# Unread TensorE products ahead of the waits in the last attention batch and ahead of the scan, with the last router logits moved

## What is computed

```python
x = x + mamba2(layernorm(x), ...)               # 64 heads of 64, state 128, convolution over 4 taps, gate, rmsnorm
x = x + cross_attention(layernorm(x), ctx, ...)  # 16 query heads of 128, 4 key heads, 64 context tokens per sequence
x = x + moe(layernorm(x), ...)                   # 8 experts, the best 2 of each token, plus 2 shared experts
```

## Time and profile before

| what | us |
| --- | --- |
| runs, median (lowest to highest, 3 runs) | 1702.9 (1699.85 to 1706.84) |
| the profiled execution, its own time | 1701.57 |
| its span, first to last instruction | 1699.8 |
| busy: TensorE products | 1608.0 |
| busy: VectorE | 1311.0 |
| busy: ScalarE | 1223.0 |
| busy: GpSimd | 601.8 |
| mean granted TensorE clock, share of full | 0.982 |

### The profile page before, as it was taken

One profiled execution on the slowest core, in us unless ns is written; L12 is line 12 of the kernel. 1 busy time (PEld: TensorE's weight loads), 2 busy tenths in 40 slices (PEclk: granted clock), 3 DMA queues, 4 the chain that ended last, 5 costly groups with the idle time before them and its releaser, 6 DMA issues. The chain is left out here.

```text
span 1699.8 us, 28898 instructions
## 1 busy us (share of the span) xinstructions
PE 1608.0 (95%) x9892; PEld 1286.0 (76%) x9892; DVE 1311.0 (77%) x2048; ACT 1223.0 (72%) x2531; POOL 601.8 (35%) x469
## 2 busy tenths in 40 slices
PE   5489999999999999999999999999968989999999
PEld 3367777777777777777777677877757889999888
DVE  7969999999999999999999865667657533333355
ACT  4679999999999999999999576566624324444331
POOL 1413343433434333333333411311121653334461
PEclk9679999999999999999999999999989999999999
DMA  8956444444444444444443100000104233223231
GB/s 321 393 226 246 171 150 173 150 153 170 151 172 149 154 169 151 166 156 155 169 152 147 56 1 1 2 1 2 47 29 146 90 131 116 90 92 112 81 94 56
DMA packets 74268, 220.30 MB, mean 130 GB/s; under 512 B 8848, under 2 KB 29584, under 8 KB 72464
## 3 DMA queue, kind: packets, MB, share of 16 engines
q1 hardware_dynamic: 68464, 192.38, 31.8%
q0 software_dynamic: 5664, 26.09, 4.4%
HBM read 184.62 MB, written 33.82 MB: 129 GB/s over the span
## 5 line engine op out<-in xcount | busy, mean ns | idle before, releaser
L624 POOL TENSOR_TENSOR m_gT<-m_gy,m_zs 128x512 f32<-128x512 f32 x128 | 166.5, 1301 | 534.4 <-DVE m_gy L794 534.4
L753 DVE SCALAR_TENSOR_TENSOR m_xc<-banks,k_cw,m_xc 128x510 f32<-128x510 f32 (+2 forms) x384 | 285.4, 743 | 15.0 <-ACT m_xc L665 5.9
L850 PE MATMUL banks<-pair_hi,m_wxz 128*128 128x512 f32 x680 | 243.5, 408 | 2.5 <-DMA m_wxz<-w_split 2.5
L893 PE MATMUL m_ps_out<-k_won,m_gT 128*128 128x256 f32 x1024 | 242.3, 379 | 3.6 <-POOL m_gT L624 2.0
L765 DVE TENSOR_TENSOR m_mat<-m_mat,k_cbm 128x768 f32<-128x768 f32 x256 | 232.5, 950 | 2.7 <-ACT m_mat L686 2.7
L893 PEld LDWEIGHTS m_ps_out<-k_won,m_gT 128*128 128x128 f32 x1024 | 193.7, 190 | 36.7 <-POOL m_gT L624 3.3
L881 PE MATMUL m_ps_y<-m_mat,m_xdt 128*64 128x256 f32 (+1 forms) x2048 | 194.7, 332 | 0.0
L686 ACT ACTIVATE m_mat<-m_mat 128x1536 f32<-128x1536 f32 x128 | 188.5, 1472 | 0.0
L881 PEld LDWEIGHTS m_ps_y<-m_mat,m_xdt 128*64 128x64 f32 x2048 | 126.8, 136 | 80.0 <-issue 42.3
L677 ACT ACTIVATE m_mat<-m_a_all,k_cum 128x256 f32<-128x256 f32 x340 | 170.5, 501 | 0.2 <-PE m_ps_y L881 0.2
L635 POOL TENSOR_TENSOR m_g_sum<-m_g_sum,m_g_sq 128x512 f32<-128x512 f32 x124 | 163.1, 1315 | 5.2 <-ACT m_g_sq L692 5.1
(11 more groups left out here) (307 smaller groups left out, 3691.5 us busy)
## 6 DMA issues: line engine op xcount, KB each, us to landing
m_wxz<-w_split SPq DMA_DIRECT2D x85, 512.0 KB, 3.4
m_a_all<-a_by_head SPq DMA_DIRECT2D x85, 512.0 KB, 4.3
k_w_first<-w_split SPq DMA_DIRECT2D x43, 512.0 KB, 3.4
k_a_first<-a_by_head SPq DMA_DIRECT2D x43, 512.0 KB, 4.3
w_split<-p_w_hl SPq DMA_DIRECT2D x15, 1024.0 KB, 8.7
raw<-in_w_gate_up POOLq DMA_DIRECT2D x9, 1280.0 KB, 6.4
raw<-in_w_xz SPq DMA_DIRECT2D x16, 512.0 KB, 7.2
raw<-in_w_down POOLq DMA_DIRECT2D x9, 640.0 KB, 7.7
```

The costliest lines, as they stand in the source:

```text
L624: pool.tensor_tensor(gT[:, n % 2, :], gy[:, n % 2, :], zs[:, n % 2, :], ALU.mult).then_inc(g_done, 1)
L753: dve.scalar_tensor_tensor(out=out[:, :, k:], in0=ps[:, :, 0:SEQ - k], scalar=cw[:, c, TAPS - 1 - k:TAPS - k], in1=out[:, :, k:], op0=ALU. ...
L850: last = pe.matmul(ps[:, :], w, a, start=m == 0, stop=m == len(terms) - 1)
L893: last = pe.matmul(ps_out[:, q * HID:(q + 1) * HID], gT[:, n % 2, q * P:(q + 1) * P], won[:, c, :], start=c == 0 and q % 2 == 0, stop=c == ...
```

## The change

TensorE's program alone is touched. In two stages it gets a helper `keep_warm(n)` that issues n products of tokens which lie in SBUF, into a PSUM tile that nobody reads again, without a semaphore. In `mamba_prepare` a product has 512 columns and goes into `ps_dt`; there are 12 of them before `c_times_b(2)`, 4 before `c_times_b(3)` and 5 after it, and ahead of the first stands a wait for both copies out of `ps_dt`. In `cross_attention_phase` a product has 256 columns and goes into `ps_q[0]`; in the last batch there are 18 before `scores(7, 1)`, 24 before `f_T(6)`, 14 before `probs_T(7, 0)` and 6 before `attend(7, 0)`. There `f_logits(6)` also moves from ahead of `probs_T(7, 1)` to behind it.

```diff
@@ mamba_prepare, tensor
+            def keep_warm(n):
+                for m in range(n):
+                    pe.matmul(ps_dt[:, 0:TG], xT_hi[:, 0, 0:P], xT_hi[:, 1, 0:TG], start=True, stop=True)
+
...
                 if m % CB == 1:
                     c_times_b(m // CB - 2)
+            pe.wait_ge(aT_done, 2)
             for g in range(2, NG):
+                keep_warm(12 if g == 2 else 4)
                 c_times_b(g)
+            keep_warm(5)
@@ cross_attention_phase, tensor
+            def keep_warm(n):
+                for m in range(n):
+                    pe.matmul(ps_q[0][:, 0:TT], xT_hi[:, 1, 0, 0:P], xT_hi[:, 1, 1, :], start=True, stop=True)
+
...
+                if not more:
+                    keep_warm(18)
                 scores(b, 1)
+                if not more:
+                    keep_warm(24)
                 if b >= 1:
                     f_T(b - 1)
                 if more:
                     q_pair(b + 1, 4)
                     q_pair(b + 1, 5)
+                else:
+                    keep_warm(14)
                 probs_T(b, 0)
                 if more:
                     scores_T(b + 1, 0)
                     q_pair(b + 1, 6)
+                else:
+                    keep_warm(6)
                 attend(b, 0)
...
-                if b >= 1:
+                if 1 <= b < NB - 1:
                     f_logits(b - 1)
...
                 probs_T(b, 1)
                 if more:
                     sum_T(b + 1)
                     scores(b + 1, 0)
+                else:
+                    f_logits(b - 1)
                 if b + 2 < NB:
                     ln_T(b + 2)
                 attend(b, 1)
```

## The result

| | before | changed |
| --- | --- | --- |
| runs, median (lowest to highest, 20 each) | 1701.43 (1698.35 to 1707.28) | 1705.9 (1702.48 to 1709.14) |
| span of the profiled execution | 1699.8 | 1703.6 |
| mean granted clock over the span | 0.982 | 0.987 |

The ratio of the runs is 1.0025, with a 95% interval of 1.0016 to 1.0033: 4.3 us slower (2.7 to 5.6), with a higher mean clock. The forecast was 1705.8 us, 2.9 us above before.

What follows compares the result with a forecast made beforehand. It took VectorE's softmax and TensorE's low clock to bound the last attention batch, and DMA stores the preparation. 0 + 2.9 on the profiled 1701.57 us gave 1704.5, plus 1.3 to the runs' median 1705.8 us; range 1700 to 1709.5.

Steps and rivals of the forecast that it cites:

- likeliest case: Whole kernel: the clock falls before `attend(7,1)` and the preparation gains nothing, 2.9 us slower in all; chance 0.65.
- The added products fit their gaps and cost nothing: Last attention batch: 18, 24, 14 and 6 products take 2.2, 3.0, 1.7 and 0.74 us inside TensorE's waits, costing 0.
- `probs_T(7,0)` and `attend(7,0)` gain 3.5 us, VectorE hides all but 1.7: Last attention batch: `attend(7,0)` ends 3.5 us earlier, but `probs_T(7,1)` waits for VectorE until 1261.75, leaving 1.7 us.
- The order takes the rest back: Last attention batch: `pT_copy(7,1)` waits behind logits and their copy, leaving a gain of 0.1 us at full clock.
- The clock falls in the gap of 2.9 us, so that `attend(7,1)` starts 1.6 us later: Between `attend(7,0)` and `probs_T(7,1)`: TensorE idles, transposes and logits run at low clock, 1.6 us later (0.8 to 2.5).
- `attend(7,1)` costs 1.3 us more, the middle of 0 and 2.6: End of last attention batch: `attend(7,1)` takes 3.72 us if the clock returns, 6.33 if not; 1.3 us more taken.
- the sum of 2.9: Last attention batch: 1.6 us later start plus 1.3 us longer `attend(7,1)`, 2.9 us later (0.8 to 6.2).
- The preparation is worth 0 because the stores cover it: End of preparation: VectorE finishes 1.5 us earlier, but SyncE's stores last to 89.2 us; 0 taken, 1.5 gained to 1.6 lost.
- rival 3: Last attention batch: added products run at low clock and become the wait, 7 us late, 1710 to 1713.6 us; chance 0.05.
- Rival 1: Last attention batch: the clock holds through the 2.9 us gap, 0.1 us earlier, 1702.8 us; chance 0.22.
- Rival 2: Preparation: stores land before VectorE is done, the block ends up to 1.5 us sooner, 1704.3 us; chance 0.08.

Runs made afterwards that it cites:

- the kernel with the logits late and all gaps filled: The changed kernel plus 22 unread products ahead of `probs_T(7,1)` and 8 behind the logits; median 1705.9 us, ratio 1.001 to the kernel before.
- the part alone: The kernel before plus only the 21 products and the wait in the preparation, nothing in the attention; median 1705.6 us, ratio 1.001 to before.
- the gap filled: The changed kernel plus 22 unread products between `attend(7,0)` and `probs_T(7,1)`; median 1706.51 us, ratio 1.0015 to the kernel before.
- the logits moved into the gap: The changed kernel with `f_logits(6)` back in its old place ahead of `probs_T(7,1)`; median 1706.71 us, ratio 1.001 to the kernel before.
- the order alone: The kernel before with only `f_logits(6)` moved behind `probs_T(7,1)` and no added product; median 1703.82 us, ratio 1.0001 to before.
- the attention alone: The changed kernel without the 21 products and the wait in the preparation; median 1706.45 us, ratio 1.001 to the kernel before.

## Why the prediction was right

Its likeliest case is what happened, and the sign, the place and the mechanism stand. By its steps:

- *The added products fit their gaps and cost nothing:* right. They took 0.13 us each (24 in 3.12 us) against 0.124, and in each of the four gaps of the attention TensorE still waited 0.4 to 0.9 us at the end.
- *`probs_T(7,0)` and `attend(7,0)` gain 3.5 us, VectorE hides all but 1.7:* right. `attend(7,0)` ended at 1257.7, which is the forecast's 1258.9 in a batch that began 1.2 us earlier, and `probs_T(7,1)` started 0.06 us after VectorE.
- *The order takes the rest back:* right at full clock, shown by the kernel with the logits late and all gaps filled: 8.23 us against 8.61, 0.4 us gained and not 0.1.
- *The clock falls in the gap of 2.9 us, so that `attend(7,1)` starts 1.6 us later:* it started 5.57 us after VectorE's end, before 3.96: 1.6 us. Of the parts, the logits took 2.74 us to ScalarE's start (2.4 taken, between 1.62 and 3.24): small products feel the clock. Their steps took 0.21 us instead of 0.11.
- *`attend(7,1)` costs 1.3 us more, the middle of 0 and 2.6:* this term was mis-sized. It cost 2.3 and 2.5 us in the two profiles: the clock fell at 1260.6 and 1259.1 us and came back only 4.8 and 5.2 us into `attend(7,1)`. That is the 1 us by which the sum of 2.9 fell short of the 3.9 in the profile.
- *The preparation is worth 0 because the stores cover it:* right for the start of the scan, which follows the stores in every profile. It came 0.7 us later than the 89.9 forecast, as the stores' last wait did; with the part alone it came at 89.79. That nothing is gained later, in the first rounds, is not settled beyond about a microsecond.
- *1705.8 us:* met within 0.1, in part by luck. The three runs of before that it started from had a median 1.5 us above that of the twenty, which made up for the short term: the loss itself was forecast at 2.9 us and measured at 4.3. In rival 3 the sum lets `attend(7,0)` take 6.8 us where the rows have 6.33; nothing else rests on it.

One step of the reasoning failed although the sum did not need it. The forecast took idle time as what decides, and counted the logits as work. With the gap filled the clock fell all the same, 4.2 us later counted from VectorE's end (9.91 us where 8.5 was expected), and with the logits moved into the gap it fell in it (9.52 where 6.8 was expected). The move had put the logits in front of the copy wait, and together they are a second stretch in which the clock can fall: it did with the gap filled, and did not with the order alone. Filling the first gap alone was not enough.

The Trainium skill's rule (TensorE: Matmul & The Clock Gate, "Why this matters for your kernels") advises against idle gaps of more than about 3 us. By that rule the gap of the change is allowed, and the change would have been worth 0.1 us. The profiles do not agree: the clock fell behind a gap of 2.87 us in the changed kernel, and with logits ahead of it 1.4 us into one of 1.64.

Rival 1 (the clock holds) did not happen in either profile of the change; the attention alone comes nearest, where the clock held for another 2.2 us behind the gap. Rival 2 (a gain in the preparation) and rival 3 (the added products at low clock) did not happen.

Open is where in each of these stretches the clock falls: in three executions with the same code in this batch (the change twice, the attention alone) it fell 0.0, 0.2 and 2.2 us behind the same gap. How often a run without the profiler is hit can't be read from these profiles. That spread, the falls in the next stage (none, 1.4, 3 and 5 us of delay to the scatter) and the time from the last scatter to the first transpose of gathered tokens (9.6 to 15.6 us, in kernels whose code there is the same) are each as large as a gain of 1.7 us in one batch, and may be why it is not seen in the times.

## What to carry to other kernels

Before filling an engine's idle time, find the wait that ends last behind it. Here a faster TensorE only met VectorE's softmax, and the time it gained turned into a new idle gap next to the very work that sets the end. Products for the sake of the clock held it only where they reached up to the last work on the path, with every wait between filled, and it is safer to count router-sized products of a few columns with the waits than with the work. And a stage's own number, taken between two fixed events in the profile, repeated within 0.2 us here, where the time of the whole kernel needs a difference of about 2.

## What was not expected of the hardware

- The clock fell with the last of twelve products of 8 columns, or within 2 us behind them, in three profiles (1264.0, 1265.1 and 1259.8 us), in one of them with TensorE "busy" 21.2 of the 24.9 us ahead of it. With eight products of 256 columns behind them, 1.2 us, it held, and in one profile (the order alone) it held without.
- Those small products take 0.21 us each at the low clock (2.35 us from the start of the first to that of the twelfth) and 0.12 at the high one (1.33 us), so their price is no fixed cost.
- A fall costs where it lands. The next stage reached its first scatter in 42.5 us in the eight profiles without one and in 43.9 to 47.6 us in the five with one or more.
